# Order of attend and score product in the unit loop of the first block's attention

## What is computed

```
def _L0_cond_ref(hidden, w, ln_g, ln_b, Wg, bg, Wb, bb, Wqkv, bqkv, Wp, bp, W1, b1, W2, b2, num_heads):
    B, N, D = hidden.shape
    hd = D // num_heads
    h = _sln(hidden, w, ln_g, ln_b, Wg, bg, Wb, bb)
    qkv = (h @ Wqkv.T + bqkv).reshape(B, N, num_heads, hd, 3)
    ...
    energy = jnp.einsum('bhqd,bhkd->bhqk', q, k)
    att = jax.nn.softmax(energy, axis=-1) / D ** 0.5
    out = jnp.einsum('bhqk,bhkd->bhqd', att, v)
    out = jnp.moveaxis(out, 1, 2).reshape(B, N, D)
    out = out @ Wp.T + bp
    h1 = out + hidden
    h2 = _sln(h1, w, ln_g, ln_b, Wg, bg, Wb, bb)
    return h2 + h1
```

## Time and profile before

| What | Value |
|---|---|
| median of 3 runs | 1681.17 us (1680.97 to 1681.72) |
| span of the profiled execution | 1679.2 us |
| TensorE busy in the span | 1642.6 us, 98% |
| VectorE, ScalarE, GpSimd busy | 49%, 41%, 26% |
| mean granted TensorE clock | 0.998 |
| unit loop of the third group | from 212.9 to 260.6 us; TensorE busy 47.4 of 47.7 us |

### The profile page before, as it was taken

One profiled execution on the slowest core, in us unless ns is written; L12 is line 12 of the kernel. 1 busy time (PEld: TensorE's weight loads), 2 busy tenths in 40 slices (PEclk: granted clock), 3 DMA queues, 4 the chain that ended last, 5 costly groups with the idle time before them and its releaser, 6 DMA issues.

```text
span 1679.2 us, 25193 instructions
## 1 busy us (share of the span) xinstructions
PE 1642.6 (98%) x8348; PEld 1248.0 (74%) x8348; DVE 824.2 (49%) x1555; ACT 688.1 (41%) x2011; POOL 432.8 (26%) x361
## 2 busy tenths in 40 slices
PE   5999999999999999999999999999999999999999
PEld 3676767676766665577777788888888888888887
DVE  4657676666757575554444562424242424242322
ACT  4657565756566553465455541212121212121210
POOL 4223223241414121533444331212121111211000
PEclk9999999999999999999999999999999999999999
DMA  6021203121212026422322440202020101010100
GB/s 236 14 70 58 90 35 112 37 94 42 83 44 81 19 88 257 150 80 91 105 100 75 145 157 1 76 1 69 6 69 6 62 12 62 12 62 12 50 0 25
DMA packets 56541, 117.23 MB, mean 70 GB/s; under 512 B 6288, under 2 KB 6288, under 8 KB 55984
## 3 DMA queue, kind: packets, MB, share of 16 engines
q1 hardware_dynamic: 56496, 116.65, 20.6%
HBM read 91.33 MB, written 25.30 MB: 69 GB/s over the span
## 4 chain that ended last, share of the span: by engine, by line
PE 89%; DMA 4%; DVE 2%; ACT 2%; issue 1%; SPq 1%; DVEq 0%; POOL 0%; ACTq 0%
PE bank L566 24%; PE bank L568 23%; PE bank L567 23%; PE bank L641 6%; PE bank L648 3%; PE bank L660 3%; DMA rows<-st_dram 2%; PE bank L592 2%; DMA xb<-x_dram 1%; PE bank L874 1%; PE bank L670 1%; PE bank L749 1%; PE bank L738 1%; DMA x_dram<-xrb 1%; PE bank L900 1%
## 5 line engine op out<-in xcount | busy, mean ns | idle before, releaser
L1187 ACT ACTIVATE gf<-bank,cols 128x512 f32<-128x512 f32 x128 | 88.0, 688 | 513.7 <-PE bank L568 513.7
L1581 DVE CAST g_hi<-gf 128x512 fp32r<-128x512 f32 x128 | 68.8, 537 | 428.3 <-ACT gf L1187 428.3
L1031 ACT ACTIVATE pa<-bank,neg_max 128x128 f32<-128x128 f32 x512 | 180.4, 366 | 74.2 <-DVE neg_max L1281 73.6
L566 PE MATMUL bank<-w_hi,g_hi 128*128 128x512 f32 x512 | 200.5, 392 | 0.0
L566 PE MATMUL bank<-hb_hi,w_hi 128*128 128x512 f32 x512 | 199.3, 389 | 0.6 <-issue 0.6
L568 PE MATMUL bank<-w_hi,g_lo 128*128 128x512 f32 x512 | 199.4, 389 | 0.0
L567 PE MATMUL bank<-w_lo,g_hi 128*128 128x512 f32 x512 | 199.2, 389 | 0.0
L568 PE MATMUL bank<-hb_hi,w_lo 128*128 128x512 f32 x512 | 199.2, 389 | 0.0
L567 PE MATMUL bank<-hb_lo,w_hi 128*128 128x512 f32 x512 | 199.2, 389 | 0.0
L1020 ACT ACTIVATE k_diag<-bank,cols 32x512 f32<-32x512 f32 x128 | 87.0, 680 | 112.5 <-PE bank L568 111.3
L641 PE MATMUL bank<-k_diag,qa 128*128 128x512 f32 x256 | 131.0, 593 | 0.0
(11 more groups left out here) (180 smaller groups left out, 3292.6 us busy)
## 6 DMA issues: line engine op xcount, KB each, us to landing
rows<-st_dram SPq DMA_DIRECT2D x32, 512.0 KB, 4.8
xb<-x_dram SPq DMA_DIRECT2D x64, 256.0 KB, 3.8
xa<-xt_in SPq DMA_DIRECT2D x32, 256.0 KB, 3.2
xra<-xt_in SPq DMA_DIRECT2D x32, 256.0 KB, 2.6
x_dram<-h SPq DMA_DIRECT2D x32, 256.0 KB, 2.5
xrb<-x_dram SPq DMA_DIRECT2D x32, 256.0 KB, 3.1
x_dram<-xrb SPq DMA_DIRECT2D x32, 256.0 KB, 2.0
xrc<-x_dram SPq DMA_DIRECT2D x32, 256.0 KB, 3.8
```

The costliest lines, as they stand in the source:

```text
L566: nc.tensor.matmul(dst, w_hi, a_hi, start=start, stop=False)
L1031: last = nc.scalar.activation(pa[:, u % 2, j, :], ps_s[u % 2][:, j * P:(j + 1) * P], ACT.Exp, bias=neg_max[:, u % 2, j:j + 1], accum_out=s ...
L1187: nc.scalar.activation(gf[f % 2][:], bank[f % 2][:], ACT.Gelu, bias=cols[:, B1_COL + f:B1_COL + f + 1])\
L1581: nc.vector.tensor_copy(g_hi[:, r, :], gf[f % 2][:]).then_inc(g_hi_ready, 1)
```

## The change

In the unit loop of `body`, `attend(g, u - 1)` is moved ahead of `scores(g, u + 2)`, directly behind `transpose_p(g, u)`.

```
                 for u in range(UNITS):
                     b, m = u // C, u % C
                     transpose_p(g, u)
+                    if u > 0:
+                        attend(g, u - 1)
                     if u + 2 < UNITS:
                         scores(g, u + 2)
-                    if u > 0:
-                        attend(g, u - 1)
                     if m == 0 and b > 0:
                         recip_t(g, b - 1)
```

## The result

The changed kernel takes 1700.06 us (median of 4 runs, 1697.14 to 1703.43) beside 1681.45 us for the kernel before (1680.97 to 1683.29). The ratio is 1.0108, with a 95% interval of 1.0093 to 1.0122. That is 18.6 us slower by the two medians and 18.2 us by the ratio (15.6 to 20.5). The forecast was 1699.1 us, 17.9 us slower.

What follows compares the result with a forecast made beforehand. TensorE, busy 98% of the span, was taken as the bound. The swap's 0.6, the waiting attends' 8.3 and the last sequences' 9.0 us sum to 17.9, so 1681.17 + 17.9 = 1699.1 us; range 1686 to 1706.

Steps and rivals of the forecast that it cites:

- What bounds the kernel: Whole kernel: TensorE is busy 98% of the span, so any time its list loses is lost at the end too.
- The swap itself: Units without other effects: attend before score product costs 0.01 us per unit, 56 times, 0.6 us in all.
- the load pulled ahead: Rival: the score product's weight load runs ahead of the attend, 0.11 us earlier at 104 places, giving 1687.7 us; chance 0.10.
- both loads exposed: Rival: both weight loads of the score product behind an attend are exposed, 104 x 0.11 us more, 1710.5 us; chance 0.07.
- score products flowing in behind attends: Rival: the score product needs neither drain nor load there, each pair gives back 0.20 us, 1678.3 us; chance 0.04.
- The chain from R to the attend: Reciprocal transposes through scale_o to attend: 2.11 us; attend waits 0.44 us at 16 places (loss 8.3 us), 1.14 at 8.
- The last sequence: Each group's last sequence: the step at line 566 starts 1.12 us later, 8 times, 9.0 us; low end 6.7.
- the prediction's two paths: To line 566's step in the last sequence: 6.90 us through row maximum and low_o, 6.62 by TensorE's own list.
- What comes late at no cost: Row maxima of swapped units come 0.55 us later without loss; at unit 4, 0.29 us of cover is left.
- The sum: All terms over the kernel: 0.6 + 8.3 + 9.0 = 17.9 us slower.

Runs made afterwards that it cites:

- Experiment 1: Attend moved ahead of the score product in every unit but 5, 9 and 13 (80 of 104 swaps), against the kernel before: 1684.66 us, ratio 1.0008.
- experiment 8: Kernel before, with attends issued in pairs at every even unit, behind the transposes and ahead of the score product: 1668.37 us, ratio 0.9915.
- experiment 7: Changed kernel, with low_o ahead of row_max on VectorE in the second unit of a sequence: 1698.25 us, ratio 1.0095 to the kernel before.
- experiment 6: Reciprocal transposes ahead of score product at sequences' first units: in the changed kernel 1702.92 us; in the kernel before, with attend ahead there too, 1687.36 us.

## Why the prediction was right, step by step

- *What bounds the kernel.* Right: TensorE's own list. Of the 16.1 us that the unit loops grew by, 12.8 are longer waits of line 660 (14.5 against 1.7 us), and the other engines' work hardly changed.
- *The swap itself, +0.01 us.* Right in the place and nearly in the size. The row that no trace of before had, S directly behind A, is there now: A to S 0.36, and S takes 0.96 to R (227.84 to 228.80) where a hidden load gives 0.87, so 0.09 to 0.10 of the load is exposed instead of 0.11. T(0) to T(4) of the third group takes 10.05 us after and 10.07 before, and the 56 swaps for which 0.6 us was forecast gave back 0.2. Experiment 1 bounds the 80 swaps that do not wait at 3 us by its time, and its rows give 0.8. This closes the rivals of the load pulled ahead, of both loads exposed, and of score products flowing in behind attends. S's load begins with S at all 104 places, where it began 0.11 us ahead of S before. So the pulling ahead that the Trainium skill describes for the reorder window (page "TensorE: Matmul & The Clock Gate", section "The mechanism") is not seen across this change of form. The page grants it to a load that does not conflict with the matmuls in flight, and no run here shows whether this one does; the rival's 1687.7 was one reading of that rule. The Trainium skill's rule that a change of tiling mode drains TensorE (page "TensorEngine Tiling (Array Packing)", section "Key Properties") agrees with the trace: with two attends in a row the second, which changes nothing, costs 0.22 us where one alone costs 0.36 (experiment 8).
- *The chain from R to the attend.* Forecast 2.11 us from R's true start, measured 2.10 to 2.11. Wait 0.44 forecast at the units 5 and 9, about 0.4 in the rows; 1.14 forecast at unit 13, 1.07 in the row. T(4) to T(6): 6.44 forecast, 6.42 measured in the third group (5.92 before); T(8) to T(10): 6.40 (5.92 before). That is 0.50 and 0.48 where 0.52 was forecast, 7.7 us in all 8 groups against 8.3.
- *The last sequence.* T(12) to P 6.90 forecast, 6.86 measured: 1.08 us a group, 8.6 us against 9.0. The part of P's wait is shown by experiment 7, 0.27 where the prediction's two paths differed by 0.28 (6.90 and 6.62).
- *What comes late at no cost.* Right as to T(4), which waited for no exponentials. At the units 4 to 6 the row maximum and `rs` meet at `scale_o`, as forecast. But the prediction treated that meeting as a matter of a tenth at one unit. It is the second chain to the same semaphore, and where R is moved ahead in the changed kernel it is the one that decides (experiment 6). For this change it made no difference. The two forecasts of experiment 6 did not count all that a pushed-back row maximum holds behind it, and missed by 12 and 6 us.
- *The sum.* From T(0) to T(15) the third group takes 46.88 us after and 44.85 before, 2.03 us more, and the eight groups together 16.1 us more, against 17.9 forecast. The interval of the ratio (15.6 to 20.5 us) holds both. The 2 us between 16.1 and the median's 18.6 are not settled: the seven stretches between the unit loops add up to between 230.7 and 233.9 us in profiled executions that have the same work and order there, and the second block varies by more still. So the mechanism and its terms were right, each a little too large, and that 17.9 lies within 1 us of the median's 18.6 is partly luck.

## What to carry to other kernels

On an engine that is busy throughout and works in a fixed order, moving one step ahead of another can cost what the other used to cover: before such a swap, look which semaphore the moved step waits for, and how far behind its last release it stands. A wait that shows 0.2 us in a few places marks a chain without reserve. Follow every list on the way to the semaphore, not only the data's path: `scale_o` needed `rs` and its own turn on VectorE, and repairing one end alone gained nothing. Steps that switch the array to another form are cheaper side by side, and the pairs also gave the waiting step its distance back.

## What the runs showed of the hardware

- Two groups of narrow products (four 32-column products each) side by side took 0.58 us to the next full-width step, one alone 0.36.
- A full-width fp32 product directly behind narrow ones took 0.09 to 0.10 us longer to the next step than behind full-width transposes; a split product's matmul pays about the same in that place (0.11). The fp32 product's weight load began 0.107 us ahead of it behind full-width transposes, and 0.001 to 0.002 us ahead of it behind narrow products, at all 104 places.
- A ScalarE copy of 128x512 to a bf16 scratch tile, 0.60 us by its row, delayed the next one by 0.49, in two kernels (24 and 8 waits of line 660 grew by that much).
- The second block took between 316 and 322 us in executions of kernels that are the same there, while the MLP took 713.4 us in each; comparisons of a few us between these kernels need many runs.
